# Three blocks of fp32r products made two in each slot of an audio tower kernel

## The chip, the cores and the metric

The kernel runs on one core of a Trainium2 chip. The metric is the device time of one execution in microseconds (us). The engines are TensorE (PE), VectorE (DVE), ScalarE (ACT), GpSimd (POOL) and SyncE (SP), each with its own queue of instructions, in order, tied together by semaphores.

## The reference

64 sequences of 750 x 128 values pass one layer of an audio tower:

```python
tokens = einsum('bnpd,edp->bne', patches, Wr) + b      # patches of 16 rows, step 8: 93 tokens
h = tokens
h = h + attn(layernorm(h))   # layernorm with gamma, beta; q, k, v = 1x1 projection, then a causal
                             # filter of 3 taps; 8 heads of 64; ALiBi bias; softmax; @ wout.T
h = h + ffn(layernorm(h))    # gate over 16 experts, top 2; per expert the mean of
                             # silu(x w1) over its tokens, times w2; mixed by the routing weights
```

## The kernel before

**Two parts.** Up to about 660 us of the profiled execution all 64 sequences (16 groups of four) are tokenised, attended and routed; each token's row is scattered to its experts' lists in HBM. After that 128-row tiles of those lists pass the expert layer, and the means are mixed into the output. The change touches the first part only.

**Step and slot.** The first part is a software pipeline of steps t = 0 to 20. In step t, group t is tokenised (`f.tok`), group t-1 gets its layer norm (`f.norm`), t-2 its projections (`f.proj`), t-3 attention (`f.attn`), t-4 the gate (`f.gate`), t-5 its scatter (`f.scat`). Steps 6 to 13 are a hardware loop over pairs of steps; the others are written out. So t = 2 has no attention yet, t = 3 to 15 have tokenising, projections and attention together, t = 16 and 17 have no tokenising, and from t = 18 on there are no projections. A step has four slots, s = 0 to 3, one per sequence of the group. The order of the work in a slot is written out by hand, for each engine separately.

**The fp32r products.** Tokenising and projecting are done with operands split in a high and a low part: `split_product` issues three matmuls (L406, L407, L408). Per slot these are four tap units, `tok_taps` (j = 0 to 3, three matmuls each, all into one PSUM bank), and three projections, `proj` with k = 3s, 3s+1, 3s+2 (three matmuls each), seven units and 21 matmuls in all. Everything else on PE is fp32 or bf16.

**PE's order in a slot before.** Transposes of the shifted scores of the sequence before (L452), transposes of v (L469; in s = 0 after projection 3s), projection 3s and tap unit 0 (first block), the product of probabilities and v, the "probT product" (L500), in s = 3 the transposes of xn (L508), bias and scores of this sequence (L516, L521: products of 64 rows, in pairs), projection 3s+1 and tap units 1 and 2 (second block), in s = 0 the transpose of rw (L536), four transposes of attn (L544), in s = 2 the gate's matmuls (L551), in s = 3 the rank's (L558 to L564), tap unit 3 and projection 3s+2 (third block), out projection (L576).

**What hangs on it.** DVE in a slot: in s = 1 and 2 the statistics of a layer norm, in s = 3 the choice of experts, then `conv` of projection 3s (L831, L834), the reciprocal and the multiply that make attn (L867, L870), the maximum of the scores and its subtraction (L876, L879), in s = 3 the rank (L925, L929), `conv` of 3s+1 and of 3s+2, the addition to resid (L891), in s = 2 the first part of the routing. ACT writes each projection's first tap (`tap2`, L675) before DVE adds the other two in `conv`; the projections alternate between two PSUM banks, so projection k waits for `conv` of k-2. ACT also makes exp (L700), copies v (L710), splits x (L667), normalises (L688) and copies attnT (L746), for which the out projection waits. POOL subtracts for x_lo (L1043) and scatters rows (L1110). The transposes of attn wait for the multiply:

```python
if prev:
    pe.wait_ge(norm_done, n)
    for j in range(QB):
        mm = nc.tensor.transpose(psV[:, j * NT:(j + 1) * NT], attn[:, j * 128:(j + 1) * 128], ident[:NT, :NT])
    mm.then_inc(a_tr, 1)
```

Of the kernel before, what the change touches and what calls it, by code (L numbers as in the profile page):

```python
# [57 lines left out]
def build(nc, x, w_tok, b_tok, gamma, beta, wq, wk, wv, cq, ck, cv, w_out, w_gate, w1, w2,  # L58
# [3 lines left out]
    with ctx:  # L62
# [192 lines left out]
        def wait(eng, s, value):  # L255

            if isinstance(value, int) and value <= 0:
                return
            eng.wait_ge(s, value)
# [143 lines left out]
        def _(pe):  # L403
# [6 lines left out]
            def tok_taps(t, s, first, count):  # L410


                if first == 0:
                    pe.wait_ge(x_lo_done, t * GB + (s + 1))
                    if isinstance(t, int) and t == 0:
                        pe.wait_ge(wtok_lo_done, s + 1)
                        pe.wait_ge(pads_ready, 4)
                    if s == 0:
                        wait(pe, tok_evac, t)
                for j in range(first, first + count):  # L420
                    at = (j // 2) * GM + j % 2
                    mm = split_product(psTok[:, 0:GM], wtok_hi[:, s, j, :], wtok_lo[:, s, j, :],
                                       x_hi[s % 2][:, at:at + GM], x_lo[s % 2][:, at:at + GM],
                                       start=(s == 0 and j == 0), stop=(s == GB - 1 and j == 3))
                if first + count == 4:
                    mm.then_inc(tap_mm, 1)
# [16 lines left out]
            def step(t, u, f):  # L443
                for s in range(GB):
# [37 lines left out]
                                                     ident[:, :])  # L482
                        mm.then_inc(tok_tr, 1)
                    if f.tok:
                        tok_taps(t, s, 0, 1)
                    if prev:

                        pe.wait_ge(p_evac, n * 2)
# [34 lines left out]
                                                      start=False, stop=True, skip_group_check=True)  # L523
                        mm.then_inc(s_mm, 1)

                    if f.proj:
                        proj(t, u, f, 3 * s + 1)
                    if f.tok:
                        tok_taps(t, s, 1, 2)
                    if f.attn and prev:  # L530
                        pe.wait_ge(v_evac, n + 1)
                    if f.scat and s == 0:
# [21 lines left out]
                    if f.gate and s == 3:  # L554


                        wait(pe, mask_done, t - 3)
                        nc.tensor.matmul(psRank[:, :], tri[:, :], mask[:, :], start=True, stop=False)  # L558
                        for b in range(GB - 1):
                            later = mask[:, b * E:(b + 1) * E].unsqueeze(1).broadcast_to([NT, GB - 1 - b, E])  # L560
                            nc.tensor.matmul(psRank[:, (b + 1) * E:].rearrange("p (b e) -> p b e", e=E), ones16[:, :NT], later,
                                             start=False, stop=(b == GB - 2))
                        for b in range(GB):
                            mm = nc.tensor.matmul(psTot, ones16[:, :], mask[:, b * E:(b + 1) * E],  # L564
                                                  start=(b == 0), stop=(b == GB - 1))
                        mm.then_inc(rank_mm, 1)
                    if f.tok:
                        tok_taps(t, s, 3, 1)
                    if f.proj:
                        proj(t, u, f, 3 * s + 2)  # L570
                    if prev:
# [88 lines left out]
        def _(ac):  # L660
# [8 lines left out]
            def tap2(t, u, k):  # L669

                wait(ac, proj_mm, (t - 2) * NBLK + (k + 1))
                if k == 0 and isinstance(t, int) and t == 2:
                    ac.wait_ge(taps_ready, 1)
                    ac.wait_ge(wqkv_lo_done, 1)
                nc.scalar.activation(qkv[u][:, k, :, :], psP[(k + 1) % 2][:, 0:GT].rearrange("p (b n) -> p b n", n=NT),  # L675
                                     ACT.Copy, scale=taps[:, k, 2:3]).then_inc(tap2_done, 1)
# [15 lines left out]
            def step(t, u, f):  # L692
                for s in range(GB):
                    n = (t - 3) * GB + s
                    prev = f.attn and s > 0 or f.last and s == 0
                    if prev:
                        wait(ac, pv_mm, n - 1)
                        for a in range(2):
                            ac.wait_ge(p_tr, n * 2 - 1 + a)
                            nc.scalar.activation(probT[:, a, :, :].rearrange("p h n -> p (h n)"),  # L700
                                                 psS[:NT, a, 0:4 * NT], ACT.Exp).then_inc(p_evac, 1)
                    if f.gate and s == 2:
                        wait(ac, hnT_tr, t - 3)
                        nc.scalar.activation(hnT[:, :], psHn, ACT.Copy).then_inc(hnT_evac, 1)
                    if f.attn:
                        ac.wait_ge(v_tr, n + 1)
                        wait(ac, pv_mm, n - 1)
                        if isinstance(t, int) and t == 3 and s == 0:
                            ac.wait_ge(vones_ready, 2)
                        nc.scalar.activation(vrow[s % 2][:, :, 0:DH],  # L710
                                             psV[:NT, :].rearrange("p (h d) -> p h d", d=DH), ACT.Copy)\
                            .then_inc(v_evac, 1)
                    if f.proj:
                        tap2(t, u, 3 * s)
                    if f.norm and s == 0:

                        wait(ac, tok_tr, t)
                        nc.scalar.activation(resid[:, bass.ds((t - 1) * (GB * D), GB * D)], psP[0][:NT, :],
                                             ACT.Copy).then_inc(res_evac, 1)
                    if f.norm and s == 3:  # L720
                        wait(ac, xnT_tr, t)
                        wait(ac, xnT_lo_done, t - 1)
                        nc.scalar.activation(xnT[:, :], psP[1][:, 0:GT], ACT.Identity, bias=bet[:, 0:1],
                                             scale=gam[:, 0:1]).then_inc(xnT_evac, 1)
                        wait(ac, xnT_evac, t)
                        nc.scalar.activation(xnT_hi[1 - u][:, :], xnT[:, :], ACT.Copy).then_inc(xnT_hi_done, 1)
                    if f.tok and f.more(t, s):
                        ac.wait_ge(x_in[(s + 1) % 2], t * (16 * GB // 2) + (16 * ((s + 1) // 2) + 16))
                        high(t * GB + (s + 1), (s + 1) % 2)
                    if f.norm and s == 2:  # L730
                        normalise(t - 1, rstd, shift, xn, ln_shift, xn_ready)
                    if f.gate and s == 1:
                        wait(ac, scattered[u], (t - u - 4) * (16 * GB))
                        normalise(t - 4, rstd2, shift2, hn[u], ln2_shift, hn_ready)
                    if f.proj:
                        tap2(t, u, 3 * s + 1)
                    if f.scat and s == 0:
                        if prev:
                            ac.wait_ge(a_tr, n)
                        else:  # L740
                            ac.wait_ge(rwT_tr, 1)
                        nc.scalar.activation(rwT[:, bass.ds((t - 5) * NT, NT)], psRT, ACT.Copy).then_inc(rwT_evac, 1)
                    if prev:
                        ac.wait_ge(a_tr, n)
                        wait(ac, out_mm, n - 1)
                        nc.scalar.activation(attnT[:, :, :].rearrange("p j n -> p (j n)"), psV[:, 0:GT],  # L746
                                             ACT.Copy).then_inc(a_evac, 1)
                    if f.gate and s == 3:
                        wait(ac, gap_done, t - 3)
                        nc.scalar.activation(egap[:, :], gap[:, :], ACT.Exp).then_inc(egap_done, 1)  # L750
                    if f.proj:
                        tap2(t, u, 3 * s + 2)
                    if isinstance(t, int) and t == 0 and s == GB - 1:
                        ac.wait_ge(proj_w_in, 16 * 8)
                        nc.scalar.activation(wqkv_hi[:, :, :], wqkv_raw[:, :, :], ACT.Copy).then_inc(wqkv_hi_done, 1)
                        ac.wait_ge(small_in, 16 * 5)
                    if f.tok and s == GB - 1:
                        wait(ac, tap_mm, t * GB + GB)
                        wait(ac, tok_tr, t)
                        nc.scalar.activation(tokT[:, :].rearrange("p (b n) -> p b n", n=NT),  # L760
                                             psTok[:, 0:GM].rearrange("p (b n) -> p b n", n=MR)[:, :, 0:NT], ACT.Identity,
                                             bias=btok[:, 0:1]).then_inc(tok_evac, 1)
# [414 lines left out]
```

## Time and profile before

| | |
|---|---|
| median of 3 runs | 823.14 us (822.13 to 823.62) |
| profiled execution | 821.97 us, its span 820.3 us |
| PE matmul busy | 742.3 us, 90% of the span |
| PE weight loads busy | 685.7 us, 84% |
| DVE busy | 615.6 us, 75% |
| ACT busy | 468.0 us, 57% |
| POOL busy | 383.2 us, 47% |

The busy shares are means over stages with different limits, so they say only which engine to look at first. What a change in a slot's order is worth has to be read from the timeline of the slots it touches. Matmuls overlap one another, so the distance from one start to the next counts, not the duration of one.

### The profile page before, as it was taken

To read this page: it belongs to the slowest core of one execution; us is meant where nothing else is said; L and a number is where in the kernel's file an instruction comes from. 1 tells how busy PE (TensorE), PEld (TensorE's weight loads), DVE (VectorE), ACT (ScalarE), POOL (GpSimd) and SP (SyncE) were. 2 spreads that over 40 slices of the span, in tenths; PEclk is the share of its full clock that TensorE was granted. 3 is DMA by queue.
4 is the path that set the end of the run, shared out by engine and by line. 5 is a ranking of instruction groups with operands and counts; after the bars stand their busy time and mean duration, and the time that the engine had idled before them with its cause. 6 is when DMAs were issued, how large, how long until landed. Compare 5 with 4: busy or idle time off the path is not lost. (4 is left out here: it accounts for less than half of the span.)

```text
span 820.3 us, 20971 instructions
## 1 busy us (share of the span) xinstructions
PE 742.3 (90%) x6670; PEld 685.7 (84%) x6670; DVE 615.6 (75%) x1621; ACT 468.0 (57%) x1021; POOL 383.2 (47%) x408
## 2 busy tenths in 40 slices
PE   5477999999999999999999999999898419999987
PEld 4466999999999999999999999998777309999983
DVE  2145788888888888888888888889986336888855
ACT  3345566656565656666566666646443108899950
POOL 3443243666555565656456565644534552222200
PEclk9798999999999999999999999999999659999989
DMA  6322123432211121112111121142000032222205
GB/s 190 105 76 54 42 67 97 135 100 52 67 50 48 47 63 51 50 47 67 51 47 47 47 71 48 32 158 77 13 13 20 20 81 73 65 64 64 64 12 149
DMA packets 42246, 53.89 MB, mean 66 GB/s; under 512 B 13651, under 2 KB 28947, under 8 KB 41680
## 3 DMA queue, kind: packets, MB, share of 16 engines
q1 hardware_dynamic: 26304, 37.13, 16.0%
q0 software_dynamic: 13120, 14.05, 6.1%
q10 hardware_dynamic: 2768, 2.00, 0.8%
q8 instruction: 32, 0.52, 0.3%
q14 instruction: 22, 0.18, 0.1%
HBM read 42.69 MB, written 10.26 MB: 65 GB/s over the span
## 5 line engine op out<-in xcount | busy, mean ns | idle before, releaser
L1110 POOL DMA_INDIRECT expert_rows<-hn,slot x128 | 167.5, 1309 | 64.3 <-issue 32.3
L1043 POOL TENSOR_TENSOR x_lo<-x_raw,x_hi 128x752 fp32r<-128x752 f32 x64 | 114.9, 1796 | 149.1 <-ACT x_hi L667 149.1
L831 DVE SCALAR_TENSOR_TENSOR qkv<-ps,taps,qkv 128x368 f32<-128x368 f32 x192 | 114.0, 594 | 76.8 <-ACT qkv L675 75.3
L675 ACT ACTIVATE qkv<-ps,taps 128x372 f32<-128x372 f32 x192 | 108.7, 567 | 87.5 <-PE ps L408 87.1
L834 DVE SCALAR_TENSOR_TENSOR qkv<-ps,taps,qkv 128x364 f32<-128x364 f32 x192 | 114.6, 597 | 6.8
L406 PE MATMUL ps<-x_hi,wtok_hi 128*128 128x376 f32 x256 | 94.5, 369 | 11.5 <-DVE wtok_lo L811 9.1
L500 PEld LDWEIGHTS psO<-vrow,probT 93*93 93x93 f32 x1024 | 93.4, 162 | 4.9 <-ACT probT L700 3.8
L500 PE MATMUL psO<-vrow,probT 93*93 93x65 f32 x1024 | 93.9, 245 | 2.2 <-ACT probT L700 1.1
L407 PE MATMUL ps<-x_lo,wtok_hi 128*128 128x376 f32 x256 | 88.3, 345 | 0.0
L408 PE MATMUL ps<-x_hi,wtok_lo 128*128 128x376 f32 x256 | 88.3, 345 | 0.0
L998 DVE TENSOR_REDUCE qkv<-qkv 128x512 f32 (+1 forms) x108 | 72.4, 681 | 18.1 <-ACT qkv L771 17.3
L406 PE MATMUL ps<-xnT_hi,wqkv_hi 128*128 128x372 f32 x192 | 77.1, 401 | 9.0 <-DVE qkv L834 4.9
L700 ACT ACTIVATE probT<-psS 93x372 f32<-93x372 f32 x128 | 54.0, 472 | 44.1 <-PE psS L452 44.1
L576 PE MATMUL psO<-wout,attnT 128*93 128x128 f32 x512 | 68.0, 276 | 8.4 <-ACT attnT L746 5.5
L576 PEld LDWEIGHTS psO<-wout,attnT 128*93 128x93 f32 x512 | 61.6, 162 | 12.1 <-ACT attnT L746 9.5
L312 POOL DMA_DIRECT2D xs<-expert_rows x54 | 29.9, 553 | 81.5 <-PE psS L595 38.8
L876 DVE TENSOR_REDUCE rmax<-psS 93x8 f32<-93x744 f32 x64 | 59.2, 926 | 7.1 <-PE psS L521 5.9
L407 PE MATMUL ps<-xnT_lo,wqkv_hi 128*128 128x372 f32 x192 | 64.2, 334 | 0.0
L408 PE MATMUL ps<-xnT_hi,wqkv_lo 128*128 128x372 f32 x192 | 64.1, 334 | 0.0
L667 ACT ACTIVATE x_hi<-x_raw 128x752 fp32r<-128x752 f32 x64 | 52.7, 824 | 19.8 <-DMA x_raw<-in_x 15.0
L879 DVE TENSOR_TENSOR shifted<-psS,rmax 93x744 f32<-93x744 f32 x64 | 59.4, 929 | 5.2
L521 PEld LDWEIGHTS psS<-qkv 64*93 64x93 f32 x1024 | 47.2, 158 | 18.2 <-issue 18.2
(160 smaller groups left out, 1607.1 us busy)
## 6 DMA issues: line engine op xcount, KB each, us to landing
x_raw<-in_x SPq DMA_DIRECT2D x64, 376.0 KB, 3.2
w1s<-in_w POOLq DMA_DIRECT2D x8, 512.0 KB, 4.8
w<-in_w SPq DMA_DIRECT2D x4, 1024.0 KB, 10.3
xs<-expert_rows SPq DMA_DIRECT2D x54, 64.0 KB, 1.8
xs<-expert_rows POOLq DMA_DIRECT2D x54, 64.0 KB, 2.1
out<-resid SPq DMA_DIRECT2D x16, 160.0 KB, 2.4
expert_rows<-hn,slot POOLq DMA_INDIRECT x128, 3.5
qkv<-in_w_tok ACTq DMA_DIRECT2D x4, 256.0 KB, 6.7
```

The lines of the kernel that those rows point to most:

```text
L406: nc.tensor.matmul(dst, w_hi, x_hi, start=start, stop=False)
L407: nc.tensor.matmul(dst, w_hi, x_lo, start=False, stop=False)
L408: return nc.tensor.matmul(dst, w_lo, x_hi, start=False, stop=stop)
L500: mm = nc.tensor.matmul(psO[:NT, h // 4, (h % 4) * (DH + 1):(h % 4 + 1) * (DH + 1)], probT[:, h % 2, h // 2, :], vrow[(s + 1) % 2][:, h, : ...
L576: mm = nc.tensor.matmul(psWout, attnT[:, j, :], wout[:, j, :], start=(j == 0), stop=(j == QB - 1))
L675: nc.scalar.activation(qkv[u][:, k, :, :], psP[(k + 1) % 2][:, 0:GT].rearrange("p (b n) -> p b n", n=NT), ACT.Copy, scale=taps[:, k, 2:3]) ...
L831: nc.vector.scalar_tensor_tensor(dst[:, :, 1:NT], src[:, :, 0:NT - 1], taps[:, k, 1:2], dst[:, :, 1:NT], ALU.mult, ALU.add).then_inc(tap1_ ...
L834: nc.vector.scalar_tensor_tensor(dst[:, :, 2:NT], src[:, :, 0:NT - 2], taps[:, k, 0:1], dst[:, :, 2:NT], ALU.mult, ALU.add).then_inc(conv_ ...
L879: nc.vector.tensor_tensor(shifted[:, :, :, :], heads(psS, NT), rmax[:, :, :].unsqueeze(3).broadcast_to([NT, 2, 4, NT]), ALU.subtract).then ...
L998: nc.vector.tensor_reduce(part[:, bass.ds(i, 1), :].rearrange("p i j -> p (i j)"), act[k][:, :].rearrange("p (j n) -> p j n", n=128), AXX, ...
L1043: nc.gpsimd.tensor_tensor(x_lo[u][:, 0:PIECE], x_raw[u][:, :], x_hi[u][:, 0:PIECE].bitcast(F32), ALU.subtract)\
L1110: nc.gpsimd.indirect_dma_start(rows, bass.IndirectOffsetOnAxis(slot[1 - u][:, c:c + 1], 0), hn[1 - u][:, c % GB, :], None)\
```

## The change

Projection 3s+1 and tap units 1 and 2 no longer stand between the scores and the transposes of attn. Tap unit 1 goes ahead, to tap unit 0; projection 3s+1 and tap unit 2 go behind the transposes (and behind the gate's and rank's matmuls), to tap unit 3 and projection 3s+2. On ACT the tap of projection 3s+1 goes behind the copies of rwT and attnT and the exp of the gap. DVE, POOL and SP keep their order. Nothing is added or removed.

```diff
@@ tensor, step
                     if f.tok:
-                        tok_taps(t, s, 0, 1)
+                        tok_taps(t, s, 0, 2)
                     if prev:
...
                         mm.then_inc(s_mm, 1)
 
-                    if f.proj:
-                        proj(t, u, f, 3 * s + 1)
-                    if f.tok:
-                        tok_taps(t, s, 1, 2)
                     if f.attn and prev:
                         pe.wait_ge(v_evac, n + 1)
...
                         mm.then_inc(rank_mm, 1)
+                    if f.proj:
+                        proj(t, u, f, 3 * s + 1)
                     if f.tok:
-                        tok_taps(t, s, 3, 1)
+                        tok_taps(t, s, 2, 2)
                     if f.proj:
                         proj(t, u, f, 3 * s + 2)
@@ scalar, step
-                    if f.proj:
-                        tap2(t, u, 3 * s + 1)
                     if f.scat and s == 0:
...
                     if f.proj:
+                        tap2(t, u, 3 * s + 1)
                         tap2(t, u, 3 * s + 2)
```

## Rows read from the trace of the kernel before

**Rows 1.** Busy time by stretch: each engine's us (instructions), PEclk granted clock.

```profile
174.00:468.00 294.00, 294.00 (x2778) 277.73 (x2776) 249.02 (x698) 179.76 (x378) 174.32 (x169) 1.00 0.20 55
543.00:612.00 69.00, 62.77 (x625) 54.57 (x624) 63.00 (x177) 36.41 (x83) 28.88 (x31) 1.00 0.22 76
...
65.00:70.00 5.00, 4.25 (x17) 3.85 (x18) 2.31 (x5) 3.04 (x5) 0.82 (x1) 0.57 0.15 60
```

**Rows 2.** Timeline, PE's matmuls: start us, duration us, count (x), idle before.

```profile
329.82 0.48 PE L516 MATMUL psS<-bias,ident 93*93 93x372 bf16 x2
...
338.91 0.90 PE L521 MATMUL psS<-qkv 64*93 64x93 f32 x16
339.74 0.44 PE L406 MATMUL ps<-xnT_hi,wqkv_hi 128*128 128x372 f32 x1
...
341.41 0.48 PE L544 MATMUL psV<-ident,attn 93*128 93x93 f32 x4
...
342.78 1.03 PE L576 MATMUL psO<-wout,attnT 128*93 128x128 f32 x8
...
347.41 0.48 PE L516 MATMUL psS<-bias,ident 93*93 93x372 bf16 x2
...
348.65 0.44 PE L406 MATMUL ps<-xnT_hi,wqkv_hi 128*128 128x372 f32 x1
...
358.23 0.44 PE L406 MATMUL ps<-xnT_hi,wqkv_hi 128*128 128x372 f32 x1
...
620.15 0.90 PE L521 MATMUL psS<-qkv 64*93 64x93 f32 x16
```

**Rows 3.** Timeline, PE's weight loads.

```profile
341.65 0.19 PEld L406 LDWEIGHTS ps<-x_hi,wtok_hi 128*128 128x128 f32 x1
...
567.70 0.19 PEld L406 LDWEIGHTS ps<-xnT_hi,wqkv_hi 128*128 128x128 f32 x1
...
575.54 0.19 PEld L406 LDWEIGHTS ps<-xnT_hi,wqkv_hi 128*128 128x128 f32 x1
...
607.32 0.36 PEld L544 LDWEIGHTS psV<-ident,attn 93*128 93x128 f32 x4 [0.83 <-issue]
607.62 0.12 PEld L558 LDWEIGHTS psO<-mask,tri 93*93 93x93 bf16 x1
...
620.98 0.36 PEld L544 LDWEIGHTS psV<-ident,attn 93*128 93x128 f32 x4
```

**Rows 4.** Timeline, DVE around the multiply (L870), and POOL.

```profile
330.12 1.79 POOL L1043 TENSOR_TENSOR x_lo<-x_raw,x_hi 128x752 fp32r<-128x752 f32 x1 [1.74 <-ACT x_hi L667]
...
330.35 0.69 DVE L870 TENSOR_TENSOR attn<-psO,rden 93x512 f32<-93x512 f32 x1
...
347.85 0.69 DVE L870 TENSOR_TENSOR attn<-psO,rden 93x512 f32<-93x512 f32 x1
...
353.15 0.60 DVE L831 SCALAR_TENSOR_TENSOR qkv<-ps,taps,qkv 128x368 f32<-128x368 f32 x1 [1.25 <-ACT qkv L675]
...
358.16 0.69 DVE L870 TENSOR_TENSOR attn<-psO,rden 93x512 f32<-93x512 f32 x1
...
606.52 0.69 DVE L870 TENSOR_TENSOR attn<-psO,rden 93x512 f32<-93x512 f32 x1
```

**Rows 5.** Timeline of t = 16, DVE and ACT.

```profile
565.81 0.69 DVE L870 TENSOR_TENSOR attn<-psO,rden 93x512 f32<-93x512 f32 x1
...
568.22 0.59 DVE L831 SCALAR_TENSOR_TENSOR qkv<-ps,taps,qkv 128x368 f32<-128x368 f32 x1
...
568.52 0.57 ACT L675 ACTIVATE qkv<-ps,taps 128x372 f32<-128x372 f32 x1
...
576.74 0.59 DVE L831 SCALAR_TENSOR_TENSOR qkv<-ps,taps,qkv 128x368 f32<-128x368 f32 x1
```

**Rows 6.** Timeline of t = 2, PE's waits.

```profile
53.75 0.43 PE L406 MATMUL ps<-xnT_hi,wqkv_hi 128*128 128x372 f32 x1 [0.78 <-DVE qkv L834]
...
64.89 0.43 PE L406 MATMUL ps<-xnT_hi,wqkv_hi 128*128 128x372 f32 x1 [3.31 <-DVE qkv L834]
```

## The prediction

> **What bounds the kernel now.** I read the page's busy shares first, then the table by stretch, then the timeline of TensorE (PE) slot by slot, and last VectorE (DVE) and ScalarE (ACT) beside it. The table [rows 1] gives three regimes. From 174 to 468 us, the hardware loop (t = 6 to 13), PE is busy 294.00 of 294.00 us: each nanosecond between two of its matmuls is a nanosecond of the kernel, and DVE (249.02) sets nothing unless PE has to wait for it. From 543 to 612 us (t = 16 and 17, no tokenising left) it is turned round: DVE is busy 63.00 of 69.00 and PE has holes. Before 75 us (t = 2) nobody is full: a chain projection, tap on ACT, two convolution steps on DVE, next projection sets the pace, and the granted clock was 0.57 between 65 and 70 us, so most of that time at the lower of its two levels, 1.2 GHz. The change acts in all three, with different signs.
>
> **What a block costs.** A fp32r block of nine matmuls took 339.74 to 341.41 = 1.67 us, and one of six 342.78 - 341.65 = 1.13 us [rows 2, 3]. The three more cost 0.54, 0.18 each; with rows rounded to 0.01, 0.173 a matmul and 0.10 us a block beside them fit both (0.10 + 9 x 0.173 = 1.66, 0.10 + 6 x 0.173 = 1.14). The removed boundary is: scores, block of nine, four transposes of attn, block of six. From the end of the scores (339.74) to the out projection (342.78) that is 3.04 us.
>
> After: scores, four transposes, block of twelve; three matmuls have gone ahead into the first block, which exists anyway. Before, the transposes' weight loads lay under the last matmul of the block: 341.41 to 341.65 = 0.24. After, they stand behind the scores. This pair is in the trace: in t = 18 there is no projection, and the scores that started at 620.15 were followed by the first load of these transposes at 620.98, 0.83 later; with a fp32r matmul behind them it is 339.74 - 338.91 = 0.83 as well [rows 2, 3]. So the pause after the scores doesn't come from the kind of number; it stays when the block goes. Uncovered, the four transposes took 607.62 - 607.32 = 0.30. New sum: 0.30 + (0.10 + 12 x 0.173) + 3 x 0.173 = 3.00. The saving is 0.04 to 0.05 us a slot, bounds 0.02 (the rows' rounding) and 0.10 (all of a block's extra). Fifty-one slots have all of it (t = 3 from s = 1, t = 4 to 15): 51 x 0.045 = **-2.3 us**.
>
> The Trainium skill, TensorEngine Tiling (Array Packing), Key Properties, says that a change of tiling mode drains TensorE. The scores are 64-row products in pairs, so by that rule too the drain stands behind them whatever follows; the two 0.83 us agree, and a reading by which the block's removal saves this drain (0.09 a slot more) is against it.
>
> **The new wait.** The transposes wait for DVE's multiply that makes attn (L870), till now hidden under the nine matmuls. From the end of a multiply to the waiting load I take 607.32 - (606.52 + 0.69) = 0.11, nearly 0.12 us. Queued behind it on PE is everything, the next projections first. Four cases, each against the end of the scores, which comes 1.24 us after the end of the probT product (347.41 to 348.65) [rows 2, 3, 4]:
>
> - s = 2: the multiply ends 347.85 + 0.69 - 347.41 = 1.13 us after the product; plus 0.12 is 1.25. It costs 0.01. This is DVE's shortest.
> - s = 1: now later than that, because DVE is still in the convolution of the slot's first projection. The product moves 0.52 us (3 x 0.173) away from that projection, DVE catches up, and it becomes the case of s = 2: 0.01.
> - s = 0: the multiply ends at 330.35 + 0.69 = 331.04, the scores at 329.82 + 1.24 = 331.06; the transpose of rw goes first and takes 0.08. It costs 0.01 to 0.02.
> - s = 3: the multiply ends at 358.16 + 0.69 = 358.85 and the scores end at 358.23. Before it DVE has the routing chain without a break, and that chain hangs on the last projection of slot 2 (353.15: it waited 1.25 us for ACT), not on the product. So the scores move 0.52 later, to 358.75, and the multiply doesn't: the wait is 358.85 + 0.12 - 358.75 = 0.21 to 0.22 us. Bounds: 0 if the chain has slack that I don't see, 0.73 if it moves along.
>
> Eight loop groups x 0.21 = 1.7. In the unrolled groups the chain has fewer semaphore steps and comes in time; for the small waits of all groups (39 slots at 0.01) I add 0.4, an estimate. Together **+2.1 us**. What waits behind: ACT's copy of attnT is early in all slots (it has twelve matmuls of time where it had six), and its tap of projection 3s+1, now behind the copy, is done before DVE reaches that convolution except by 0.4 us in s = 1, where DVE later waits less. The gate's and rank's matmuls only come earlier. SP's and POOL's queues issue the same DMAs; x's buffers come free with the last tap, whose distance to the slot's end is kept. I cost these at nothing; the cover is DVE's idle time in the loop, 294 - 249 = 45 us in 32 slots, 1.4 each.
>
> **The last two groups.** Here no taps exist, so nothing moves ahead into the first block, DVE sets the pace, and projection 3s+1 moves from under DVE's multiply to behind the transposes. In s = 2 the gate's matmuls stand before it too. With N the end of the multiply (565.81 + 0.69 = 566.50): the load of the transposes at N + 0.12, transposes 0.30, gate 0.6, projection's first load at N + 1.05; load to ACT's tap took 568.52 - 567.70 = 0.82, the tap 0.57, so the convolution can start at N + 2.47. Before it started at 568.22 = N + 1.72 [rows 3, 5]. DVE has nothing else in its order: +0.75. In s = 3 the rank's matmuls stand before it: load 575.54, tap at 576.36, done 576.93, convolution 576.97 for 576.74: +0.23. In s = 0 about +0.1. In s = 1 the tap of 0.57 leaves ACT's queue ahead of the attnT copy, so the out projection and the next slot's softmax come earlier: +0.2 in t = 16, -0.5 in t = 17, where DVE waits for ACT. Two groups: 1.5 + 0.46 + 0.2 - 0.3 = **+1.9 us**, bounds +0.8 (s = 2 at half of it) and +2.5 (no gain in s = 1).
>
> **The start.** In t = 2 PE waited 0.78 us for DVE before projection 4 and 3.31 before projection 9 [rows 6]. Projection 3s+2 stands twelve matmuls (2.1 us) behind 3s+1; after, nine, and the fourth tap unit fills the hole ahead of 3s+1 instead. That is 0.52 us off the chain up to three times, but DVE's own pace of two steps of 0.6 per projection takes some back; following the chain, projection 9 comes 0.8 earlier. In s = 3 the extra tap unit delays the xn transposes by up to 0.5 and one tap unit fewer stands before projection 11; at the lower clock (0.57 in the row) that unit is about 0.9. Sum: 0.8 - 0.2 + 0.9 = **-1.5 us**. Bounds: -0.8 (the first part alone) and -2.6, if the shifted work keeps the clock at 2.4 GHz through 65 to 72 us.
>
> **Sum.** -2.3 + 2.1 + 1.9 - 1.5 = +0.2. The profiled execution took 821.97 us (span 820.3 and 1.7 around it); it becomes 822.2. The median of the runs shown is 823.14, 1.17 above it; so 823.3.
>
> **Rivals.**
>
> *DVE late in every slot (slower).* While POOL's subtraction for x_lo runs (330.12 for 1.79 us), the multiply started later and ended 330.35 + 0.69 - 329.82 = 1.22 after the product instead of 1.13 [rows 2, 4]: 0.09. The product moves 0.52 towards that subtraction. In s = 1 and 2 it should still miss it, by 0.2 to 0.4 us; if the multiply falls behind it, both slots lose 0.09 in twelve groups: 24 x 0.09 = 2.2, time 825.5. It decides from where the multiply starts after x_lo's subtraction. For it: margins are thin, and any lateness now counts in full. Against: 1.13 is met in the only slots where DVE is free. Chance 0.26.
>
> The Trainium skill, SBUF — State Buffer, Who interferes with whom, says that a DVE instruction with at most one SBUF input outside the two-port modes does not contend with GpSimd. The multiply has one input in PSUM, one in SBUF; by that rule the 0.09 would be none and the rival void; the row with 1.22 speaks against taking it so.
>
> *The end is not DVE's (faster).* If DVE in t = 16 and 17 has slack in its order that I count as busy, the +1.9 falls away: 821.4. For it: it idles 6 of 69 us there. Against: in its order the maximum and the subtraction stand between N and the convolution at N + 1.72, and they fill that time. Chance 0.15.
>
> *The block was free (no change in the loop).* If the transposes' loads are pulled into the scores' pause, each slot saves 0.10 more: 5 us, 818.3. The load at 620.98 says no. Chance 0.02.
>
> **How the numbers follow.** My forecast has 0.57. A measurement of this kernel tells about 0.2%, 1.6 us, from no change. Range 821.2 to 826.0: below, the start at its best or the end at half; above, the late multiply with 0.5 over. Faster by over 0.2%: 0.16; within: 0.58; slower: 0.26.
>
> **What would show it.** After the scores at once the transposes, 0.83 after the scores' start in s = 0, 1, 2 of the loop; a wait on DVE's multiply of 0.2 us in s = 3; a block of twelve of 2.2 us; the loop longer by less than 1 us over eight groups. In t = 16 and 17, DVE idle 0.7 us before the second convolution of s = 2. Before 75 us, the scores of t = 3 some 1.5 us earlier. The prediction is wrong if the wait for the multiply shows in s = 1 or 2, or if the start doesn't move.

## The result and the profile after

The changed kernel took 827.07 us in the median of 11 executions (825.69 to 829.77), the kernel before 824.66 us on the same chip (11 executions, 822.04 to 826.68). The ratio is 1.0038, with a 95% interval of 1.0022 to 1.0055: slower, by about 3.1 us. The forecast was 823.3 us, range 821.2 to 826.0; of the 3.8 us between them 1.5 are the kernel before itself, whose three runs shown ahead of the forecast had a median of 823.14 us. The kernel was timed twice more, on the chips of the later runs, and gave 1.0011 [0.9993, 1.0029] and 1.0032 [1.0016, 1.0047]. The profiled execution took 826.35 us, its span was 824.7, against 821.97 and 820.3.

**The loop** went nearly as worked out. By stretch, at the same places as [rows 1] (us; PE, weight loads, DVE, ACT, POOL; then the granted clock):

```profile
175.00:469.00 294.00, 292.74 (x2775) 277.65 (x2776) 252.64 (x698) 178.68 (x378) 174.62 (x169) 1.00 0.21 55
65.00:70.00 5.00, 4.25 (x15) 3.88 (x16) 2.12 (x4) 1.84 (x4) 0.00 (x0) 0.50 0.15 57
```

PE was busy for all 294 us of the loop before, and for 292.74 now: the missing 1.26 us are the new wait. It stands in the timeline of PE (slots s = 0, 2 and 3 of a loop group), and in that of its weight loads (s = 2 and 3):

```profile
330.94 0.48 PE L516 MATMUL psS<-bias,ident 93*93 93x372 bf16 x2
331.35 0.90 PE L521 MATMUL psS<-qkv 64*93 64x93 f32 x16
...
332.32 0.48 PE L540 MATMUL psV<-ident,attn 93*128 93x93 f32 x4
...
348.44 0.48 PE L516 MATMUL psS<-bias,ident 93*93 93x372 bf16 x2
348.85 0.90 PE L521 MATMUL psS<-qkv 64*93 64x93 f32 x16
...
358.39 0.90 PE L521 MATMUL psS<-qkv 64*93 64x93 f32 x16
359.45 0.51 PE L540 MATMUL psV<-ident,attn 93*128 93x93 f32 x4 [0.16 <-DVE attn L867]
```

```profile
349.68 0.36 PEld L540 LDWEIGHTS psV<-ident,attn 93*128 93x128 f32 x4
...
359.42 0.36 PEld L540 LDWEIGHTS psV<-ident,attn 93*128 93x128 f32 x4 [0.29 <-issue]
```

In s = 0 (behind the transpose of rw) and s = 2 the transposes follow the scores at once. In s = 3 PE waits for the multiply, and DVE says why:

```profile
331.47 0.69 DVE L867 TENSOR_TENSOR attn<-psO,rden 93x512 f32<-93x512 f32 x1
...
348.88 0.69 DVE L867 TENSOR_TENSOR attn<-psO,rden 93x512 f32<-93x512 f32 x1
...
356.79 0.29 DVE L911 TENSOR_TENSOR hot<-misc,idxf 93x128 f32<-93x128 f32 x1
357.11 0.22 DVE L915 TENSOR_TENSOR mask<-hot 93x64 bf16<-93x64 f32 x1
357.25 0.59 DVE L828 SCALAR_TENSOR_TENSOR qkv<-ps,taps,qkv 128x368 f32<-128x368 f32 x1
357.88 0.60 DVE L831 SCALAR_TENSOR_TENSOR qkv<-ps,taps,qkv 128x364 f32<-128x364 f32 x1
358.39 0.20 DVE L864 RECIPROCAL rden<-psO 93x8 f32<-93x8 f32 x1
358.62 0.69 DVE L867 TENSOR_TENSOR attn<-psO,rden 93x512 f32<-93x512 f32 x1
```

The routing chain and the convolution run up to the multiply without a hole. It ends at 359.31; the scores, 0.83 long, at 359.22; with 0.12 from DVE to PE the load can stand at 359.43, and the weight load is at 359.42, 1.03 after the scores' start for 0.83 in s = 2. From one slot's scores to the next's, as means over 31 steps of t = 7 to 14: before 8.67, 8.89, 9.58, 9.50 (36.64 a group), after 8.63, 8.84, 9.53, 9.68 (36.69). Three slots gain 0.03 to 0.05 each, and the fourth gives it back.

**The last two groups.** DVE and ACT in t = 16, s = 2, and PE's loads beside them, each its own fence of the timeline:

```profile
566.26 0.69 DVE L867 TENSOR_TENSOR attn<-psO,rden 93x512 f32<-93x512 f32 x1
...
569.45 0.60 DVE L828 SCALAR_TENSOR_TENSOR qkv<-ps,taps,qkv 128x368 f32<-128x368 f32 x1 [0.70 <-ACT qkv L673]
```

```profile
567.06 0.36 PEld L540 LDWEIGHTS psV<-ident,attn 93*128 93x128 f32 x4 [0.51 <-issue]
567.36 0.74 PEld L547 LDWEIGHTS psO<-wgate,hnT 128*93 128x93 f32 x8
568.02 0.19 PEld L406 LDWEIGHTS ps<-xnT_hi,wqkv_hi 128*128 128x128 f32 x1
```

With N = 566.26 + 0.69 = 566.95: load of the transposes N + 0.11, projection N + 1.07, convolution N + 2.50, DVE idle 0.70. The prediction had N + 0.12, N + 1.05 and N + 2.47; before it was N + 1.72 [rows 5]. PE's scores, after and then before:

```profile
549.87 0.90 PE L521 MATMUL psS<-qkv 64*93 64x93 f32 x16
...
615.91 0.90 PE L521 MATMUL psS<-qkv 64*93 64x93 f32 x16
```

```profile
549.41 0.90 PE L521 MATMUL psS<-qkv 64*93 64x93 f32 x16
...
613.77 0.90 PE L521 MATMUL psS<-qkv 64*93 64x93 f32 x16
```

From the first scores of t = 16 to those of t = 18 it is 615.91 - 549.87 = 66.04 us, before 613.77 - 549.41 = 64.36: **+1.68 us**.

**The start.** PE's timeline before 76 us, after and then before; rows of the same work beside those of [rows 6]:

```profile
46.45 0.68 PE L406 MATMUL ps<-xnT_hi,wqkv_hi 128*128 128x372 f32 x1 [3.71 <-POOL xnT_lo L1095]
...
49.34 0.52 PE L406 MATMUL ps<-x_hi,wtok_hi 128*128 128x376 f32 x1
50.08 0.33 PE L406 MATMUL ps<-xnT_hi,wqkv_hi 128*128 128x372 f32 x1
...
54.35 0.33 PE L406 MATMUL ps<-xnT_hi,wqkv_hi 128*128 128x372 f32 x1
...
64.87 0.68 PE L406 MATMUL ps<-xnT_hi,wqkv_hi 128*128 128x372 f32 x1 [3.30 <-DVE qkv L831]
...
67.84 0.83 PE L508 MATMUL ps<-ident,xn 93*128 93x93 f32 x4
...
75.46 0.35 PE L469 MATMUL psV<-ident,qkv 128*93 128x128 f32 x1 [1.10 <-DVE qkv L831]
```

```profile
47.03 0.44 PE L406 MATMUL ps<-xnT_hi,wqkv_hi 128*128 128x372 f32 x1 [3.22 <-POOL xnT_lo L1098]
...
48.95 0.44 PE L406 MATMUL ps<-xnT_hi,wqkv_hi 128*128 128x372 f32 x1 [0.18 <-ACT resid L718]
...
66.32 0.82 PE L508 MATMUL ps<-ident,xn 93*128 93x93 f32 x4
...
74.72 0.68 PE L469 MATMUL psV<-ident,qkv 128*93 128x128 f32 x4 [1.42 <-DVE qkv L834]
```

From projection 1 to projection 4 it is shorter, as foreseen: 54.35 - 50.08 = 4.27 us, before 53.75 - 48.95 = 4.80. But two things stood against it that the sum had not. A second tap unit now stands ahead of projection 1, in a stretch at the lower clock (a matmul of 0.52 where 0.34 is usual): projection 1 starts 1.13 us later, from an earlier projection 0. And the xn transposes start 2.97 after projection 9, for 1.43: the extra tap unit, again at the lower clock. Projection 9 starts at 64.87 for 64.89, not 0.8 sooner, and the first transpose of v in t = 3 comes 0.74 us later. These two executions also differ in their granted clock, 0.84 between 44 and 55 us after and 1.00 before, so part of that is not the order; profiles at the same clock are compared further down.

**Behind the last scores** stands the largest piece, 2.06 us of it in a part that the change doesn't touch: from the last scores to the first of the last eight scatters (L1107, DMA_INDIRECT) 24.63 us before, 25.99 after, and 0.7 further on. The table by stretch, first before, then after:

```profile
633.56:658.19 24.63, 10.52 (x95) 9.03 (x94) 10.28 (x54) 4.36 (x12) 11.96 (x12) 0.68 0.07 17
```

```profile
635.89:661.88 25.99, 12.52 (x95) 10.77 (x94) 10.29 (x54) 4.47 (x12) 11.98 (x12) 0.59 0.07 16
```

The same 95 matmuls take 12.52 for 10.52 us; DVE's and POOL's sums are the same. The granted clock was 0.59 for 0.68: PE had been set back to 1.2 GHz sooner. Whether that belongs to the change, or only to this execution, was the question the runs had to answer.

### The profile page after: what moved, and what is told of

Same layout as the page of the kernel before. It is cut to its first block and busy times, and to the rows that moved or that the text cites. A ratio compares the mean times of both kernels' runs of the same rounds, so it can differ in the third digit from the quotient of the medians.

```text
span 824.7 us, 20971 instructions
## 1 busy us (share of the span) xinstructions
PE 743.6 (90%) x6670; PEld 688.9 (84%) x6670; DVE 621.7 (75%) x1621; ACT 466.9 (57%) x1021; POOL 383.7 (47%) x408
## 5 line engine op out<-in xcount | busy, mean ns | idle before, releaser
L1107 POOL DMA_INDIRECT expert_rows<-hn,slot x128 | 168.2, 1314 | 64.8 <-DVE slot L948 32.4
L406 PE MATMUL ps<-x_hi,wtok_hi 128*128 128x376 f32 x256 | 90.3, 353 | 12.0 <-DVE wtok_lo L808 9.0
```

What stands on the lines that cost most here:

```text
L406: nc.tensor.matmul(dst, w_hi, x_hi, start=start, stop=False)
L1107: nc.gpsimd.indirect_dma_start(rows, bass.IndirectOffsetOnAxis(slot[1 - u][:, c:c + 1], 0), hn[1 - u][:, c % GB, :], None)\
```

## The experiments

All edits use one plan: for each group t (the loop's count as a middle one) and slot s it says whether the old order stands there, and how many tap units go ahead of the scores.

```diff
-                        tok_taps(t, s, 0, 1)
+                        tok_taps(t, s, 0, ahead(t, s))
...
-                    if f.proj:
+                    if f.proj and middle(t, s):
                         proj(t, u, f, 3 * s + 1)
-                    if f.tok:
-                        tok_taps(t, s, 1, 2)
+                    if f.tok and middle(t, s):
+                        tok_taps(t, s, ahead(t, s), 3 - ahead(t, s))
...
+                    if f.proj and not middle(t, s):
+                        proj(t, u, f, 3 * s + 1)
                     if f.tok:
-                        tok_taps(t, s, 3, 1)
+                        last = 3 if middle(t, s) else ahead(t, s)
+                        tok_taps(t, s, last, 4 - last)
```

ACT's tap of projection 3s+1 follows the same rule. All of them do the whole computation. Each was timed against the kernel before on its chip, mostly in 12 executions.

**One stretch at a time.** The new order only in t <= 2, only in t = 3 to 15, only from t = 16 on:

```diff
+            return not (k <= 2)
```
```diff
+            return not (3 <= k <= 15)
```
```diff
+            return not (k >= 16)
```

> The new order only in t = 0 to 2, the old one from t = 3 on. In the traces of before and after, the transposes of v of t = 3 started at 74.72 and 75.46 us: 0.74 later, where the prediction had 1.5 earlier. Theory A (the order itself costs there: the extra tap unit ahead of projection 1 and of the xn transposes runs at the lower clock level and is longer than what the shorter way from 3s+1 to 3s+2 gives back): 0.5 to 1.5 us slower than before in the mean, the v transposes of t = 3 at 75 us or later in the trace. Theory B (the clock's level in one execution made the difference, the order is neutral or better there as predicted): 0 to 1.5 us faster, the v transposes anywhere between 73 and 75.5 according to the granted clock. In both, the hardware loop's length is unchanged from before.

> The new order only in t = 3 to 15, the old one before and after. Between the traces the scores of t = 15, s = 3 lie 0.26 us nearer to those of t = 3, s = 0. Both theories: 0.3 us faster than before, not to be told from no change; per slot -0.04 to -0.05, and +0.16 to +0.21 at each s = 3 of the loop. A rival (the rest of the slowdown comes from the loop by a way that the trace of one execution hides): 1 to 2 us slower.

> The new order only from t = 16 on, which changes something in t = 16 and 17 alone. Theory (VectorE waits there for the tap of projection 3s+1): the scores of t = 18, s = 0 come 1.7 us later, measured from the scores of t = 15, s = 3; time 1.7 us slower than before. The rest of the difference between the two profiled executions, 2.1 us after the last scores, went with the clock (at its lower level for 44 us instead of 38): if it is tied to the later end of the attention, this kernel shows it too and is 3 to 4 us slower; if it is chance of one execution, 1.7.

Measured: start 0.9985 [0.997, 1.0001], middle 1.0002 [0.9984, 1.002], last groups 1.0014 [0.9996, 1.0032]. In the start's profile the first transpose of v came 0.50 us sooner. The middle's profile shows its slots as in the changed kernel (36.69 a group) and a span of 825.8 us all the same: it ran at a mean clock of 0.952, its transposes of v in t = 3 came 1.93 us later than before although nothing ahead of them had changed, and from the last scores to the first of the last eight scatters it lost another 2.3. That is the size of what one execution can differ by at a lower clock. In the last groups, t = 16 to t = 18 took 66.78 us.

**Two stretches at a time, and the whole again.**

> The new order only from t=3 on; t<=2 in the old one. Theory A: the middle's +0.2 and the last groups' +1.2 to +2 remain: ratio 1.001 to 1.003. If the start is what costs in the changed kernel (its first v transposes of t=3 came 0.74 us later than before): this kernel is faster than the changed one by 0.7 us or more. If the start still gains (the start alone gave 0.9985): slower than the changed one by about 1 us.

> The new order for t<=15, the last groups in the old one. If the last two groups carry the loss (1.7 us between the first scores of t=16 and those of t=18 in the changed kernel's profile): 1.2 to 2 us faster than the changed kernel, ratio to before 0.998 to 1.0005, and t=16 to t=18 take 64.36 us as before. If the loss is the clock behind the last scores whatever the order of the groups: the ratio stays at that of the changed kernel.

> The changed kernel itself, against the kernel before, on the chip of the three runs that follow. Theory A (the terms are local and add up: start, loop groups, last two groups; the rest of the +3.1 us of the first comparison was the granted clock behind the last scores, which does not belong to the change): the ratio is that of the three parts alone, about +0.2 to +1.5 us (1.000 to 1.002), and in the profile the time from the last scores of t=18 to the first of the last eight scatters is anywhere between 24.6 and 26.9 us. Theory B (the whole costs more than its parts, because the order in t<=2 and t>=16 shifts when the clock falls): +3 us again (1.003 to 1.005), lower clock from about 640 us, and 26 us or more for that stretch. Theory C (the change costs nothing beyond chance): 1.000 or less.

> The changed kernel once more, since the two comparisons so far gave 1.0038 and 1.0011. Over all executions the span went up by 0.49 us for each 0.001 that the mean granted clock was lower. Theory A (the change costs about 1 us at equal clock and, beside it, 0.5 to 1 us because it runs at a slightly lower clock more often): ratio 1.001 to 1.003, span at a mean clock of 0.957 of 823.9 to 824.6 us against 822.9 for the kernel before, and again nearly no execution with a mean clock of 0.960 or more (1 of 23 so far, 26 of 70 for the kernel before). Theory B (the lower clock was chance): the clocks are spread as those of the kernel before and the ratio is 1.001.

Measured: from t = 3 on 1.0011 [0.9992, 1.003]; up to t = 15 0.998 [0.9962, 0.9998]; the changed kernel again 1.0011 and 1.0032. With the old order kept in t = 16 and 17 the stretch from t = 16 to t = 18 took 64.40 us again, and the ratio was in the range forecast for the case that these groups carry the loss. The kernel with the old start had the ratio of the whole, so neither of the two forecasts on the start (0.7 us faster, 1 us slower) came. Single profiles can't separate these kernels, since the same kernel's span moves by 6 us with the clock. But each execution has its span and its mean granted clock, 194 of them over these six kernels and the kernel before. One least-squares fit to all of them (span = a + a term for each stretch in the new order + a term for the clock) gives:

| term | us | standard error |
|---|---|---|
| kernel before, at a mean clock of 0.957 | 822.88 | 0.05 |
| new order in t <= 2 | -0.01 | 0.11 |
| new order in t = 3 to 15 | -0.19 | 0.12 |
| new order from t = 16 on | +1.37 | 0.11 |
| mean clock lower by 0.001 | +0.49 | 0.01 |

The three add up to +1.2 us at equal clock. The fit takes for granted that the terms add, and the errors leave differences between chips out (the kernel before lay 0.3 us higher on one chip than on another at equal clock). With a term for each kernel instead, the same fit gives -0.44 for the start alone, -0.44 for t = 3 to 15 alone, +0.92 for the last groups alone, +0.93 from t = 3 on, -0.48 up to t = 15 (0.17 each) and +1.27 (0.11) for the whole. The three alone add up to +0.04. So what the whole costs at equal clock is measured, 1.2 to 1.3 us, and most of it needs the last groups; that the parts simply add is not shown, and single terms are known to about 0.4 us.

In plain means: 35 executions of the changed kernel had a span of 824.87 us at a clock of 0.9557, 99 of the kernel before, on three chips, 822.68 at 0.9576. Of these 2.2 us the 0.0019 of clock are 0.9. On the two chips that have clocks of both the difference is 2.0 us, with the same 0.0019. So of the second timing's theories each of A and B holds in part: the last groups carry most of the loss, as A had it, and the changed kernel runs at a lower clock more often, as B had it. For the third timing theory A holds nearly (the ratio, 1.0032, lies just above its range; the span at a clock of 0.957, 824.3, inside it). The spread is not that of the kernel before: 2 of 35 executions had a clock of 0.960 or more, for 47 of 99; on those two chips, 2 of 24 for 36 of 64.

**The start at the same clock.** Seven profiles have the old order in t <= 2, six the new one in all its slots. Set side by side by their granted clock between 44 and 55 us, and counted from projection 0 (us):

| | old order, clock 1.00 (2) | old order, 0.84 (5) | new order, 0.84 (6) |
|---|---|---|---|
| projection 0 to projection 4 | 6.72 | 7.86 to 7.90 | 7.76 to 7.93 |
| projection 0 to projection 9 | 17.86, 17.90 | 19.01 to 19.07 | 18.40 to 18.45 |
| projection 9 to the transposes of xn | 1.28, 1.43 | 2.03, 2.04 | 2.91 to 2.98 |
| projection 9 to the first transpose of v | 9.82, 9.83 | 10.59 | 10.59 in four, 9.05 and 9.13 in two |

At the same clock projection 9 comes 0.6 us sooner with the new order, where 0.8 was forecast; up to projection 4 nothing is gained, since projection 1 starts later by as much as the way from it is shorter. Behind projection 9 the unit moved ahead costs 0.9 us at the transposes of xn, and the unit taken away behind them gives the same 0.9 back: 10.59 us with either order where the granted clock stayed at 0.50 to 0.57 between 65 and 75 us. The two profiles with 9.05 and 9.13 had 0.83 there. The kernel before was profiled in one of the two executions with the clock up.

**Behind the last scores.** From the last scores to the first of the last eight scatters it took 24.63 to 26.91 us in the eight profiles with the old order in t = 16 and 17 (24.63 in three of them), and 25.99 to 26.60 in the six with the new one. So the 1.36 us of the two first profiles are within what unchanged code does; whether the change has a share in them stays open.

**The clock in t = 17.** Part of the lower clock has a place. In four of the six profiles with the new order in t = 16 and 17 the clock fell for some microseconds inside t = 17; in none of the eight with the old order there. With the last groups alone, and in the changed kernel where it didn't fall:

```profile
608.00:614.00 6.00, 4.75 (x43) 4.58 (x40) 4.95 (x11) 1.71 (x4) 0.00 (x0) 0.72 0.00 0
610.10:613.50 3.40, 3.40 (x22) 3.36 (x20) 2.42 (x6) 1.69 (x4) 0.00 (x0) 0.50 0.00 0
```

```profile
608.00:614.00 6.00, 3.93 (x37) 3.52 (x38) 5.67 (x14) 2.49 (x6) 0.00 (x0) 1.00 0.00 0
```

The step from the last scores of t = 17 to those of t = 18 is then 9.6 us for 8.8. Ahead of it PE had more holes than before: over all its matmuls of t = 17 it was idle 4.77 us of 33.06 in the changed kernel, 3.65 of 32.39 before, with the clock up in both. The five kernels with the new order there and a kernel before on the same chip ran at a mean clock 0.0013 lower than it, the seven others 0.0001 lower; a single one of these means is uncertain by 0.001. That the wider holes are what brings the clock down fits all this; no run tried it by itself. The Trainium skill, TensorE: Matmul & The Clock Gate, Part 1, says that a monitor of how busy PE is sets its clock; the 0.50 in a stretch behind wider holes agrees.

**Three tap units ahead in s = 3** (t = 3 to 15; otherwise as the middle alone):

```diff
+            return 1 if middle(t, s) else 3 if s == 3 else 2
```

> As middle_only, but in s = 3 of t = 3 to 15 three tap units stand ahead of the probabilities' product instead of two. Theory (the wait of 0.16 to 0.21 us in s = 3 of the loop is for VectorE's multiply, whose time hangs on the last projection of slot 2, not on the product): the scores come 0.52 us later, the multiply doesn't, the wait is gone, and the loop shortens by 0.045 in each slot: 51 x 0.045 = 2.3 us faster than before. Rival (the multiply moves along with the product): the wait stays and the kernel is as middle_only, 0.3 us faster.

Measured: 1.0023 [1.0009, 1.0037], 36.76 us a group. PE's timeline in s = 3, then DVE's:

```profile
359.30 0.90 PE L530 MATMUL psS<-qkv 64*93 64x93 f32 x16
360.13 0.54 PE L553 MATMUL psV<-ident,attn 93*128 93x93 f32 x4
```

```profile
359.03 0.69 DVE L884 TENSOR_TENSOR attn<-psO,rden 93x512 f32<-93x512 f32 x1
360.25 0.93 DVE L890 TENSOR_REDUCE rmax<-psS 93x8 f32<-93x744 f32 x1 [0.54 <-PE psS L530]
```

The wait for the multiply is gone, as the theory had it, but the 2.3 us are not won: the kernel is slower than the middle alone (1.0002), by 0.07 us in a loop group and 0.3 to 0.5 in t = 3 to 5. DVE, which until then had no hole in this slot, now idles 0.54 us for the scores that were pushed back. That its later work then reaches PE late is argued, not tried.

**One tap unit ahead** (t = 3 to 15; the blocks joined, the taps' part of the change left out):

```diff
+            return 1
```

> The blocks joined in t=3 to 15, but with one tap unit ahead of the scores as before, not two; the other three stand in the joined block. This takes the taps' part of the change away. Theory: the 0.52 us of the second tap unit is what lets DVE finish the slot's first convolution and its multiply in time. Without it the wait for the multiply in s=3 grows to 0.2 us or stays there, and in s=1 one of up to 0.5 us comes: 0.3 to 0.7 us a group over the changed order, +4 to +9 us for the whole, ratio 1.004 to 1.010. Rival (DVE has that slack in any case, and the second tap unit matters nothing): the loop's groups as in the changed kernel, 36.69 us each, ratio 1.000.

Measured: 833.11 us for 823.53, ratio 1.0108 [1.0087, 1.0128], 37.45 us a group. PE's timeline in s = 1 and s = 3, and what the waits list from 112 to 550 us (us in total, times, longest):

```profile
345.28 0.51 PE L553 MATMUL psV<-ident,attn 93*128 93x93 f32 x4 [0.26 <-DVE attn L884]
...
364.40 0.43 PE L553 MATMUL psV<-ident,attn 93*128 93x93 f32 x3 [0.70 <-DVE attn L884]
```

```profile
PE psV L553 <- DVE attn L884: 9.2, 19, 0.7
```

In the changed kernel the same line of the waits is:

```profile
PE psV L540 <- DVE attn L867: 1.4, 8, 0.2
```

So the second tap unit ahead of the scores is what makes the joined block bearable at all: it is worth 0.52 us in s = 3 and 0.27 in s = 1, 0.76 a group.

**The old order kept in s = 3.**

```diff
+            return not (k <= 2 or (k <= 15 and s != 3))
```

> As the run before, but the step s=3 of t=3 to 15 keeps the old order as well, so that nothing stands ahead of its scores but one tap unit and the multiply has the middle block's time. Theory (the loop's group pays 0.13 to 0.20 us at s=3 for the wait for the multiply and gains 0.04 to 0.06 in each of three other slots): no wait at s=3, about -0.14 us for a group, first scores of t=3 to last of t=15 shortened by 1.7 to 2.2 us against before (0.26 in the changed kernel); time 822 to 823 us where before has 824.7, ratio 0.997 to 0.999. Rival (VectorE sets the pace of every slot, so what three slots give is waited for in the fourth): the stretch is within 0.4 us of before, ratio about that of the run before this one.

Measured: 0.9982 [0.9964, 0.9999], 36.51 us a group, 0.13 less than before. PE's timeline in s = 3:

```profile
356.61 0.90 PE L530 MATMUL psS<-qkv 64*93 64x93 f32 x16
357.44 0.44 PE L415 MATMUL ps<-xnT_hi,wqkv_hi 128*128 128x372 f32 x1
...
359.11 0.48 PE L553 MATMUL psV<-ident,attn 93*128 93x93 f32 x4
```

The nine matmuls cover the multiply again, no wait of PE is listed from 330 to 480 us, and the gain of the three other slots stays: 13 x 0.13 = 1.7 us. At a mean clock of 0.957 the executions lie 1.7 us under those of the kernel before (821.16 for 822.88). The rival, that VectorE takes back in the fourth slot what three gave, falls.

**The old order in every s = 3 up to t = 15, the first groups too.**

```diff
+            return not (k <= 15 and s != 3)
```

> The new order for t<=15 except in every s=3, that of the first groups too. In t=2, s=3 the extra tap unit stood ahead of the xn transposes and, at the lower clock, took 0.9 us of their time. Theory (this is what ate the start's gain of 0.5 us at each of projections 4 and 7): the xn transposes come 1.4 us behind projection 9, not 3.0, the first v transposes of t=3 come 0.5 to 1 us sooner than in the kernel with s=3 old from t=3 on alone, and the time is 0.5 us below it: ratio 0.996 to 0.998. Rival (the wait before projection 11 is DVE's own pace, whatever PE does): no difference from that kernel, 0.998.

Measured: 821.76 us, the ratio 0.9979 [0.9965, 0.9992], the best of all. Its reason did not hold. The xn transposes came 2.04 us behind projection 9, not 1.4 (2.03 is what the old order has at this clock, 1.4 what it has at the higher one), and from projection 9 to the first transpose of v it took 9.72 us, where the kernel of the run before took 9.13: that one was mostly at 2.4 GHz there (0.34 for a matmul of the taps), this one at 1.2 for longer (0.52). At equal clock it is 0.4 us (with 0.2 of uncertainty) under that kernel. The order of s = 3 in the start is left open.

**The old order in s = 2 of the last groups** (and the new one from t = 16 on otherwise):

```diff
+            return not (k >= 16 and s != 2)
```

> The new order for t=16 and later alone, but with the old order in every s=2. Theory (in s=2 the projection that was moved now stands behind DVE's multiply, the transposes and the gate's matmuls, and the second convolution starts 0.75 us later): the step from the scores of s=2 to those of s=3 in t=16 is 7.77 us as before, not 8.54, the one in t=17 7.44, not 7.88; from the first scores of t=16 to those of t=18 1.2 us less than with the new order in all slots, so about +0.5 us against before, and the ratio 0.5 to 1 us below that of the last groups alone (1.0014). Rival (ScalarE or the output chain sets the pace there, and the later convolution only takes slack): the stretch is as long as with all slots new.

Measured: 1.0008 [0.9995, 1.0022]. The steps from s = 2 to s = 3 are 8.17 and 7.34 us; all slots new gave 8.55 and 7.88. So the moved projection of s = 2 costs 0.38 us in t = 16 and 0.54 in t = 17, not 0.75; what is left of the 0.78 in t = 16 comes from the slot before. ACT's timeline in this kernel, then before:

```profile
567.15 1.66 ACT L700 ACTIVATE xn<-resid,shift,rstd 93x128 f32<-93x128 f32 x4 [2.37 <-POOL shift L1090]
```

```profile
565.95 1.65 ACT L688 ACTIVATE xn<-resid,shift,rstd 93x128 f32<-93x128 f32 x4 [1.55 <-POOL shift L1076]
```

The normalisation's xn starts 1.06 us after the scores (566.09) for 0.59 (565.36), since behind an s = 1 in the new order the last statistics (L859, L845) start 1.19 us ahead of the scores on DVE instead of 1.65, and POOL's chain hangs on them; ACT's next tap (568.71 for 567.51) stands behind it. The whole stretch took 65.84 us with the clock down at its end (9.60 for that step, 8.81 without), some 65.0 without: 1.0 less than all slots new, for 1.2 expected.

## Why the prediction was wrong

- **What a block costs: right.** 0.04 to 0.05 us a slot was forecast, and three slots of four gained 0.03 to 0.05. The transposes' load stands 0.83 behind the scores' start (349.68 - 348.85). The Trainium skill's rule of the drain (TensorEngine Tiling (Array Packing), Key Properties) agrees with the trace here: the pause stayed where the block went.
- **The new wait: right in place and size.** 0.21 for s = 3 only; the load came 1.03 behind the scores for 0.83, 0.20. Three tap units ahead removed it, one brought 0.7. For t = 3 to 15 the sum had -0.2, the trace has -0.26 from the first scores of t = 3 to the last of t = 15, and the fit -0.19 (-0.44 where the order is new in these groups alone).
- **The rival of the late multiply: did not come, and its reading of the rows was wrong.** In s = 2 the multiply ended 348.88 + 0.69 - 348.44 = 1.13 after the product, as before; in s = 0 of the loop, 331.47 + 0.69 - 330.94 = 1.22, again as before. But POOL's subtraction does not make the 0.09 by itself. In t = 4, s = 0 of the changed kernel it runs as well, and the multiply ends 111.74 + 0.69 - 111.30 = 1.13 after the product:

```profile
111.30 0.48 PE L516 MATMUL psS<-bias,ident 93*93 93x372 bf16 x2
```

```profile
111.74 0.69 DVE L867 TENSOR_TENSOR attn<-psO,rden 93x512 f32<-93x512 f32 x1
```

```profile
111.05 1.78 POOL L1040 TENSOR_TENSOR x_lo<-x_raw,x_hi 128x752 fp32r<-128x752 f32 x1 [3.90 <-ACT x_hi L665]
```

The later start (0.32 to 0.46 us behind the reciprocal's, 0.22 to 0.24 elsewhere) stands in s = 0 of the eight loop steps and of t = 14, not in t = 4, 5 and 15; what makes it is open. The Trainium skill (SBUF — State Buffer, Who interferes with whom) says that a DVE instruction with at most one SBUF input does not contend with GpSimd outside the two-port modes; these rows agree with it, and the prediction's reading of the 1.22 against it was wrong.
- **The last two groups: the mechanism right, the size nearly.** +1.9 was the term; the profile's stretch grew by 1.68, the fit gives +1.37 (+0.92 with the last groups alone). In t = 16 the single steps fit (N + 2.47 was forecast and N + 2.50 measured, +0.75 and +0.78). In t = 17, s = 2 it was +0.43 and not +0.75, and s = 1 gave 0.07 where 0.5 was forecast; these two misses nearly cancel. And a part of what was put on the projection in s = 2 came over the normalisation chain from s = 1, as the last run shows.
- **The start: the step that failed.** The term was -1.5, with bounds of -0.8 and -2.6; the fit has -0.01 (0.11), the start alone -0.44 (0.17). Of its three parts the first, 0.8 up to projection 9, held nearly: 0.6 at the same clock, though the tap unit ahead of projection 1, which the sum priced at nothing, took back the whole gain up to projection 4. The other two, -0.2 and +0.9, did not. The unit moved ahead of the xn transposes was priced at 0.2, the unit taken away behind them at 0.9, the second alone at the lower clock in full; they are the same three matmuls in the same stretch, and measured 0.9 each way, together nothing while the clock stayed down. Against the profile of the kernel before, with its clock up in this stretch, even the 0.6 disappeared. The bound towards zero should have been a loss: nothing in the rows excluded it.
- **A term that the sum lacked: the granted clock.** The sum started from one profiled execution of the kernel before, whose clock of 0.962 was the highest that this kernel reached in any execution on record, and took the clock as given. The changed order ran 0.0019 lower in the mean, 0.9 us. The last groups' wider holes are the likely source of a part of it; the rest is open, and chance in the executions is not excluded for it.

So of the +2.2 us in the plain means against +0.2 of the sum, by the fit's terms 1.5 is the start, 0.9 the clock, and -0.5 the last groups. The first comparison lay another 0.9 above this, within its interval. The rival of the faster end (821.4) was wrong too: DVE waited there for what was moved, 0.70 us in one slot. The third rival, in which the transposes' loads are pulled into the scores' pause, did not come either: the load stood 0.83 behind the scores' start.

## What to carry to other kernels

Before two blocks are joined, look at what the block between them covered: here nine matmuls hid a multiply in the one slot of four in which VectorE has no slack, and a change that keeps the old order just there kept the gain (ratio 0.9979) that the uniform change lost. The same edit in a loop, a fill and a drain is three changes; cost each by its own bottleneck, and where a term comes out of a chain followed, let its bound reach over zero. Where a unit of work is moved within a stretch, price it at the same clock where it arrives and where it leaves. Compare kernels that differ by a microsecond through many executions with their granted clock beside them, not through one profile each.

## What the runs showed of the hardware

- One kernel's span moved by 6 us between executions with its mean granted clock: the kernel before had 820.3 us at 0.962 and 826.7 at 0.950 (means of 18 and 3 executions), and all kernels together 0.49 us for each 0.001.
- Lower-clock stretches don't stand at fixed places of the program. In the seven kernels with the same order up to there, from projection 0 to the first transpose of v in t = 3 it took 27.7 us in the two profiles with a granted clock of 1.00 between 44 and 55 us, and 29.6 to 29.7 in the five with 0.84.
- In t = 4, s = 0 POOL's subtraction (128x752, 1.78 us) did not hold up DVE's multiply with one PSUM and one SBUF input: the multiply ended 1.13 us after the product under it and without it.
- Holes that were wider by a microsecond in 33 us (4.77 idle for 3.65) went with a fall to 1.2 GHz inside t = 17 in four of six profiles, and in none of eight without them; no run tried the cause by itself.
